# A token mixer on one core: softmax division moved behind the weighing of the values, and the work lists of three engines laid anew

## The chip, the core and the metric

The kernel runs on one core of one Trainium2 chip, in one launch. Its time is the device time in microseconds (us). The profile of one execution gives, for each engine, when every instruction ran and what it waited for. TensorE is called PE, VectorE DVE, ScalarE ACT, GpSimd POOL, and SyncE, which only starts transfers here, SP.

## The reference, cut to what matters

All data is float32. 16 images become 64 tokens each, 32 text tokens are set behind them (N = 96 tokens of D = 192 numbers, 16 samples), and two layers follow. The first has an attention with 12 heads of 8 numbers, within 4 segments of 24 tokens:

```python
qb, kb, vb = (blk(q), blk(k), blk(v))          # (B, H, SPLIT, seg, hd)
scores = jnp.einsum('bhsqd,bhskd->bhsqk', qb, kb) * scale
attn = jax.nn.softmax(scores, axis=-1)
ob = jnp.einsum('bhsqk,bhskd->bhsqd', attn, vb)
o = ob.transpose(0, 2, 3, 1, 4).reshape(B, N, C1)
return o @ W_proj + b_proj
```

Behind it come a residual sum, a layer norm and a mixture of 8 experts (192 to 768 to 192, two experts a token, a capacity for each expert). The second layer has a linear attention with L1 norms and a soft mixture of 8 experts with 4 slots each.

## The kernel before

**Staging.** The 1536 tokens are worked on in four rounds j = 0 to 3 of four samples (384 tokens, three blocks of 128). The stages follow one another on PE: patch embedding with the first attention (to about 123 us), the eight experts (to 246.5 us), the sums over experts and layer 1 (to the end). In the first and the last stage the rounds overlap: while round j's softmax runs on DVE and ACT, PE projects round j+1.

**Order.** There is no scheduler. Each engine has a list of calls, written out by hand (PE's begins at L917, ACT's at L1298, DVE's at L1866, POOL's at L450), and works it off strictly in that order. Calls wait for one another by semaphores; in PE's list the lines `free(name=count)` are such waits. A call that waits holds up everything behind it on its engine.

**The first attention, round j.** `turn_inputs` and `reduce_inputs` bring the normalised tokens in front of the projections `queries`, `keys`, `values`. `scores(j)` (L640) gives the logits of all 12 heads in three PSUM banks, one for each group g of four heads. DVE's `score_max(j, g)` subtracts the largest logit, ACT's `exp_scores(j, g)` takes the exponential, and DVE's `score_norm(j, g)` (L1541, L1543, L1545) adds up each row, takes the reciprocals of the sums and multiplies the weights by them. Then PE turns the weights (`turn_weights`, L647), ACT copies them to SBUF (`keep_weights`, L1208), and PE multiplies them with the values (`weigh_values(j, g)`, L658): 16 products of 24 columns for each g, all of one g into the same 32 rows of PSUM bank 3. ACT's `keep_outputs(j)` (L1213) copies the result, `project(j)` (L669) projects it, and DVE's `add_attention(j)` (L1568) adds it to the residual stream.

**Routing.** From there DVE works out each token's experts (`route_moments`, `route_logits`, `choose_first`, `choose`), PE counts the tokens of each expert (`count_choices`), DVE places them (`place`, L1625) and writes one-hot matrices (`mark_slots`, L1648), and PE's `dispatch` (L692) and `dispatch_tails` (L707) gather the experts' inputs. Only when all four rounds are dispatched does PE begin the experts (L718).

**Dummies.** `keep_busy` (L509) multiplies the identity with constants into a bank that is free. Four calls stand ahead of the experts, behind `dispatch(0)`, `turn_weights(3, 1)` and `count_choices(3)` (two); others stand in layer 1. The clock of PE can fall when it idles, and they fill waits.

**Transfers.** SP starts the weights of the first three experts in 12 pieces, each behind a number of subtractions of `score_max`; the later ones follow as buffers come free.

Of the kernel before, what the change touches and what calls it, by code (L numbers as in the profile page):

```python
# [5 lines left out]
ALU = mybir.AluOpType  # L6
# [3 lines left out]
AX_X = mybir.AxisListType.X  # L10
# [20 lines left out]
J, NB, QB = 4, 3, 32  # L31
# [58 lines left out]
def build(nc, xin, xhalo, txt, wtok, wtok2, lnw, lnb, tokbias, consts, wred, bred, wqkv0, bqkv0, wproj0, bproj0,  # L90
          wrouter, wi, wo, wq1, wkv1, wproj1, bproj1, slots, lscale, wdown, bdown, wup, bup, out):
    with ExitStack() as ctx:  # L92
# [68 lines left out]
        ssum = sb("ssum", [128, NGRP, 4 * GRP])  # L161
# [212 lines left out]
        def _(gp):  # L374
# [32 lines left out]
            for b in range(4):  # L407
                then(gp.memset(qmask[QB * b:QB * b + QB, b:b + 1], 1.0))
            for a in (0, 64):
# [79 lines left out]
        def _(pe):  # L489
# [154 lines left out]
            def turn_weights(j, g):  # L644
                pe.wait_ge(sem("a_prob"), NGRP * j + g + 1)
# [279 lines left out]
            square_sums(1)  # L925
# [7 lines left out]
            reduce_inputs(0)  # L933
            patches(2, 1)
# [7 lines left out]
            square_rows(3)  # L942
            free(tok_mid=4, tok_var=4)
            scores(0)
            turn_inputs(1)
            free(tok_mid=6, tok_var=6)
            patches(3, 0)
            free(a_sub=3)
            turn_projection()
            free(a_xnT=2)  # L950
            reduce_inputs(1)
# [3 lines left out]
            square_sums(3)  # L955
            turn_weights(0, 0)
            route_projection()
            queries(1)
            free(tok_mid=8, tok_var=8)
            values(1)  # L960
            free(a_kexp=8, a_qT=2)
            turn_inputs(2)
            free(a_vexp=9)
            turn_weights(0, 1)
# [6 lines left out]
            free(a_probT=2)  # L971
            weigh_values(0, 0)
            weigh_values(0, 1)
            weigh_values(0, 2)
# [8 lines left out]
            turn_weights(1, 0)  # L983
            turn_weights(1, 1)
            free(a_sub=6)
            scores(2)
            free(a_probT=5)
            weigh_values(1, 0)
            turn_inputs(3)
            free(a_vexp=27)  # L990
            count_choices(0)
            free(a_probT=4)
            turn_weights(1, 2)
            weigh_values(1, 1)
            weigh_values(1, 2)
            free(a_xnT=4)
            reduce_inputs(3)
            free(a_oT=2)
            project(1)
            free(a_h=2, r_part=2)  # L1000
            turn_weights(2, 0)
            free(r_counted=1)
            values(3)
            turn_weights(2, 1)
            queries(3)
            free(a_xl=4, a_xrT=4)
            keys(3)
            free(a_probT=8)
            weigh_values(2, 0)
            weigh_values(2, 1)  # L1010
            free(a_sub=9)
            scores(3)
            turn_weights(2, 2)
            free(a_vexp=36)
            count_choices(1)
            weigh_values(2, 2)
# [3 lines left out]
            free(r_counted=2)  # L1020
            free(xeT=2)
            keep_busy(0, 512)
# [19 lines left out]
            keep_busy(0, 384)  # L1042
            keep_busy(0, 256)
# [17 lines left out]
            combine(2, 0)  # L1061
            linear_keys_values(0, 0)
            linear_queries(0)
            linear_keys_values(0, 1)
            turn_linear(1)
# [6 lines left out]
            linear_keys_values(1, 1)  # L1072
            linear_outputs(0)
            linear_keys_values(1, 2)
            key_products(1)
            combine(3, 1)
            linear_queries(1)
            linear_project(0, 0)
            turn_linear(2)
            key_sums(1)  # L1080
# [7 lines left out]
            key_sums(2)  # L1088
            turn_linear(3)
            soft_logits(0)  # L1090
            linear_project(1, 0)
# [5 lines left out]
            linear_outputs(2)  # L1097
            turn_soft(1)
            linear_keys_values(3, 2)
            soft_logits(1)  # L1100
            linear_project(2, 0)
            linear_project(2, 1)
            linear_queries(3)
            soft_inputs(1)
            key_sums(3)
            key_products(3)
            keep_busy(0, 512, 2)
            linear_outputs(3)
            turn_soft(2)
            linear_project(3, 0)  # L1110
            soft_logits(2)
            linear_project(3, 1)
            soft_inputs(2)
            keep_busy(0, 256)
# [8 lines left out]
            soft_hidden(3, 4)  # L1123
            slot_outputs(2)
            token_outputs(0)
# [7 lines left out]
        def _(act):  # L1133
# [75 lines left out]

            def keep_outputs(j):  # L1210
                act.wait_ge(sem("a_oT_ps"), j + 1)
                need(act, "a_proj_ps", j - 2)
                nc.scalar.copy(oT[0:C1, j % 3].rearrange("c (x b t) -> c x b t", x=NB, b=4),  # L1213
# [934 lines left out]
```

## Time and profile before

| | |
|---|---|
| median of 3 runs | 353.9 us (352.41 to 355.89) |
| the profiled execution, its own time | 353.93 us |
| its span, first to last instruction | 352.1 us |
| PE busy | 329.2 us (93%) |
| DVE busy | 204.2 us (58%) |
| ACT busy | 100.9 us (29%) |
| POOL busy | 50.5 us (14%) |
| granted clock of PE, mean | 0.993 |

Busy time counts compute instructions only. A float32 product is two instructions in the trace. The groups of instructions name a line, an engine, the tiles, the shape, the count, the busy time, the mean of one in ns, and the idle time just before them with what ended it. A granted clock of 1.00 is 2.4 GHz, 0.50 is 1.2 GHz.

### The profile page before, as it was taken

The numbers are of one execution on the slowest core, as the hardware profiler recorded it, in microseconds if no ns is written. First come the engines' busy times: TensorE is split into PE (matmuls) and PEld (weight loads), VectorE is DVE, ScalarE is ACT, GpSimd is POOL, SyncE is SP. The second block draws the span as 40 slices with busy tenths as digits, with TensorE's granted clock in tenths as the row PEclk, the third lists the DMA queues.
The fourth block names the chain that finished last, engine by engine and source line by source line (L and its number), as shares of the span: only waits on it lengthen the run. The fifth ranks groups of instructions, "written<-read, shape, count | busy, mean of one in ns | idle before, by whom it ended". The sixth has DMA issues, their size and how long they took to land. (4 is left out here: it accounts for less than half of the span.)

```text
span 352.1 us, 7993 instructions
## 1 busy us (share of the span) xinstructions
PE 329.2 (93%) x3292; PEld 234.9 (67%) x3292; DVE 204.2 (58%) x639; ACT 100.9 (29%) x210; POOL 50.5 (14%) x119
## 2 busy tenths in 40 slices
PE   3899999998799899999999999999999999997975
PEld 3676567786574458678595867758867675775564
DVE  5936388999988952243325324332525476888545
ACT  1233557876433510101011010101021234322440
POOL 8604252332111020000000000000111020110100
PEclk9999999999999999999999999999999999999989
DMA  7993010522600029993487130000000000000005
GB/s 257 345 234 104 4 58 17 136 77 63 159 16 1 2 54 197 186 238 85 143 193 169 38 98 0 3 0 3 0 2 0 2 2 0 3 2 0 2 1 134
DMA packets 27804, 26.65 MB, mean 76 GB/s; under 512 B 4118, under 2 KB 22936, under 8 KB 27768
## 3 DMA queue, kind: packets, MB, share of 16 engines
q1 hardware_dynamic: 26871, 25.55, 29.0%
q10 hardware_dynamic: 896, 0.59, 0.7%
q8 instruction: 26, 0.43, 0.5%
q14 instruction: 11, 0.08, 0.1%
HBM read 24.86 MB, written 1.28 MB: 74 GB/s over the span
## 5 line engine op out<-in xcount | busy, mean ns | idle before, releaser
L736 PEld LDWEIGHTS banks<-sb_wo_sl,sb_attn_hidT_attn 128*128 128x128 f32 x384 | 62.2, 190 | 5.6 <-issue 4.9
L736 PE MATMUL banks<-sb_wo_sl,sb_attn_hidT_attn 128*128 128x192 f32 x384 | 64.5, 328 | 0.0
L1714 DVE COPY sb_w_tok_e_out<-banks 60x384 f32<-60x384 f32 x32 | 17.8, 555 | 49.8 <-PE banks L736 49.3
L1242 ACT ACTIVATE sb_attn_hidT_attn<-banks 128x480 f32<-128x480 f32 x24 | 13.6, 571 | 102.9 <-PE banks L723 102.9
L718 PE MATMUL banks<-sb_tok_xeT,sb_wi_sl 128*128 128x480 f32 x96 | 40.1, 567 | 1.1 <-ACT sb_tok_xeT L1227 1.1
L1704 DVE TENSOR_SCALAR sb_attn_hidT_attn<-banks 128x480 f32<-128x480 f32 x24 | 15.8, 658 | 27.9 <-PE banks L723 25.9
L718 PEld LDWEIGHTS banks<-sb_tok_xeT,sb_wi_sl 128*128 128x128 f32 x96 | 18.0, 190 | 18.9 <-issue 17.0
L503 PE MATMUL banks<-sb_tok_xeT 128*32 128x193 f32 (+1 forms) x512 | 24.8, 328 | 0.0
L723 PE MATMUL banks<-sb_tok_xeT,sb_wi_sl 64*128 64x480 f32 x96 | 21.5, 580 | 0.0
L503 PEld LDWEIGHTS banks<-sb_tok_xeT 128*32 128x32 f32 (+1 forms) x512 | 16.8, 109 | 6.5 <-issue 3.6
L474 POOL MEMSET sb_attn_hidT_attn<- 1x384 f32 x1 | 0.4, 413 | 119.6 <-PE banks L736 119.6
L779 PE MATMUL banks<-sb_w_kv,sb_xnT 96*128 96x384 f32 x48 | 17.3, 493 | 0.0
L756 PE MATMUL banks<-sb_w_tok_e_out,sb_onehot_combT 128*64 128x192 f32 x192 | 16.9, 329 | 0.1
L723 PEld LDWEIGHTS banks<-sb_tok_xeT,sb_wi_sl 64*128 64x128 f32 x96 | 8.6, 186 | 12.3 <-issue 12.3
L756 PEld LDWEIGHTS banks<-sb_w_tok_e_out,sb_onehot_combT 128*64 128x64 f32 x192 | 13.3, 137 | 3.2 <-issue 1.0
L658 PEld LDWEIGHTS banks<-sb_attn_hidT_attn 128*32 128x32 f32 x384 | 12.4, 113 | 2.9 <-ACT sb_attn_hidT_attn L1208 1.8
L1488 DVE BATCH_NORM_STATS2 sb_stat<-sb_h 128x6 f32<-128x192 f32 x48 | 14.0, 347 | 0.3
L658 PE MATMUL banks<-sb_attn_hidT_attn 128*32 128x24 f32 x384 | 13.2, 190 | 0.8 <-ACT sb_attn_hidT_attn L1208 0.8
L1141 ACT ACTIVATE sb_onehot_combT<-sb_tok_xeT 128x1024 f32<-128x1024 f32 x8 | 8.3, 1054 | 15.8 <-DMA sb_tok_xeT<-in_xhalo 15.8
L520 PE MATMUL banks<-sb_w_tok_e_out,sb_ln_b 128*128 128x192 f32 x30 | 7.3, 404 | 5.4 <-DMA sb_w_tok_e_out<-in_wtok 5.4
L242 PE MATMUL banks<-sb_cst,sb_attn_hidT_attn 128*128 128x128 f32 (+1 forms) x72 | 10.8, 280 | 1.7 <-DVE sb_logits L1571 1.2
L779 PEld LDWEIGHTS banks<-sb_w_kv,sb_xnT 96*128 96x128 f32 x48 | 8.5, 190 | 4.7 <-issue 0.4
(239 smaller groups left out, 540.1 us busy)
## 6 DMA issues: line engine op xcount, KB each, us to landing
sb_wo_sl<-in_wo SPq DMA_DIRECT2D x16, 288.0 KB, 4.1
sb_tok_xeT<-in_xin SPq DMA_DIRECT2D x8, 448.0 KB, 6.0
sb_onehot_combT<-route_rows SPq DMA_DIRECT2D x6, 512.0 KB, 8.8
sb_wi_sl<-in_wi SPq DMA_DIRECT2D x8, 288.0 KB, 3.4
sb_wi_sl<-in_wi SPq DMA_DIRECT2D x24, 96.0 KB, 3.4
sb_xn<-route_rows SPq DMA_DIRECT2D x4, 512.0 KB, 11.3
sb_w_tok_e_out<-in_wtok SPq DMA_DIRECT2D x2, 960.0 KB, 7.3
sb_attn_hidT_attn<-route_rows SPq DMA_DIRECT2D x2, 512.0 KB, 12.2
```

Source lines behind the costliest of these rows:

```text
L242: return nc.tensor.transpose(dst, src, ident[0:rows, 0:rows])
L503: nc.tensor.matmul(PS[QB * b:QB * b + QB, bank, at:at + D + 1], x_k[0:rows, (2 * j + b // 2) % NX, t, cols], w_eff[0:rows, t], start=(t == ...
L658: mm = nc.tensor.matmul(PS[g * 32:g * 32 + 32, 3, at:at + SEG], v_exp[:, j % 2, b, s, g * 32:g * 32 + 32], probT[:, g, b, s * 32:s * 32 + ...
L718: nc.tensor.matmul(PS[:, HID_BANKS[f], 0:SLOTS], wi_sl[:, q, f * 128:(f + 1) * 128], xeT[:, 0, e].rearrange("k g c -> k (g c)"), start=Tru ...
L723: nc.tensor.matmul(PS[:, HID_BANKS[2 * n + z], 0:SLOTS], wi_sl[rows, q, F + n * 128:F + (n + 1) * 128], xeT[rows, 1, e].rearrange("k g c - ...
L736: mm = nc.tensor.matmul(PS[:, 4 + j // 2, j % 2 * D:(j % 2 + 1) * D], hidT[:, e % 2, f, j * 128:(j + 1) * 128], wo_sl[:, q, f], start=(f = ...
L756: mm = nc.tensor.matmul(PS[rows, comb_bank(j, part), blk % 2 * D:(blk % 2 + 1) * D], combT[:, NB * j + blk, ep, rows], e_out[:, 2 * j + hf ...
L779: mm = nc.tensor.matmul(PS[:, 2 + blk, 0:2 * D], xnT[:, kh, blk * 128:(blk + 1) * 128], w_kv1[:, kh], start=(kh == 0), stop=(kh == 1))
L1242: nc.scalar.activation(hidT[:, e % 2, f].rearrange("f (g c) -> f g c", g=PAIRS)[:, :, 0:CAP], PS[:, HID_BANKS[f], 0:SLOTS].rearrange("f (g ...
L1488: ve.bn_stats(stat6[:, blk], h[:, j, blk]).then_inc(sem("stat6"), 1)
L1704: ve.tensor_scalar(hidT[:, e % 2, f].rearrange("f (g c) -> f g c", g=PAIRS)[:, :, 0:CAP], PS[:, HID_BANKS[f], 0:SLOTS].rearrange("f (g c) ...
L1714: ve.tensor_copy(e_out[64 * (e % 2):64 * (e % 2) + CAP, hf * 4 + z:hf * 4 + z + 3:2, e // 2], PS[64 * z:64 * z + CAP, 4 + hf, 0:2 * D].rea ...
```

## The change

1. **Division behind the weighing.** `score_norm` is gone. PE turns the bare exponentials (`turn_weights` waits for `a_exp`). `weigh_values(j)` first multiplies a new constant `head_ones` (128x32; ones where a row belongs to a head's keys) with the turned weights: three products of 384 columns, one for each g, which give each head's sum in PSUM bank 2, in the layout of the outputs. DVE's new `sum_scales(j)` takes the reciprocal of these 96x384 numbers, and `keep_outputs(j)`, now on DVE, multiplies the outputs by it while it copies them.
2. **Three head groups in one step.** `weigh_values(j)` waits once for all three groups, and its 48 products go over g innermost, so that three neighbours write different 32 rows.
3. **No dummies ahead of the experts.** The four `keep_busy` calls there are gone.
4. **Orders laid anew** on PE, ACT and DVE, in both layers. DVE gets one more wait, for `keys(1)`, ahead of `token_rows(6)`. POOL sets `head_ones` up (five fills).

```diff
-            def weigh_values(j, g):
-                if g == 0:
-                    pe.wait_ge(sem("a_vexp"), 9 * j + 9)
-                    pe.wait_ge(sem("a_vexp_late"), 2 * SEGS * (j + 1))
-                pe.wait_ge(sem("a_probT"), NGRP * j + g + 1)
+            def weigh_values(j):
+                pe.wait_ge(sem("a_vexp"), 9 * j + 9)
+                pe.wait_ge(sem("a_vexp_late"), 2 * SEGS * (j + 1))
+                pe.wait_ge(sem("a_probT"), NGRP * j + NGRP)
+                for g in range(NGRP):
+                    mm = nc.tensor.matmul(PS[g * 32:g * 32 + 32, 2, 0:TOK], head_ones[:],
+                                          probT[:, g].rearrange("k b (s t) -> k b s t", s=SEGS)[:, :, :, 0:SEG],
+                                          start=True, stop=True)
+                mm.then_inc(sem("a_total_ps"), 1)
                 for b in range(4):
                     for s in range(SEGS):
                         at = b * N + s * SEG
-                        mm = nc.tensor.matmul(PS[g * 32:g * 32 + 32, 3, at:at + SEG], v_exp[:, j % 2, b, s, g * 32:g * 32 + 32],
-                                              probT[:, g, b, s * 32:s * 32 + SEG], start=True, stop=True)
-                if g == NGRP - 1:
-                    mm.then_inc(sem("a_oT_ps"), 1)
+                        for g in range(NGRP):
+                            rows = slice(g * 32, g * 32 + 32)
+                            mm = nc.tensor.matmul(PS[rows, 3, at:at + SEG], v_exp[:, j % 2, b, s, rows],
+                                                  probT[:, g, b, s * 32:s * 32 + SEG], start=True, stop=True)
+                mm.then_inc(sem("a_oT_ps"), 1)
...
-            def score_norm(j, g):
-                n = NGRP * j + g
-                ve.wait_ge(sem("a_exp"), n + 1)
-                ve.tensor_reduce(ssum[:, g], prob_view(j, g), AX_X, ALU.add).then_inc(sem("a_sum"), 1)
-                ve.wait_ge(sem("a_sum"), 2 * n + 1)
-                ve.reciprocal(ssum[:, g], ssum[:, g]).then_inc(sem("a_sum"), 1)
-                ve.wait_ge(sem("a_sum"), 2 * n + 2)
-                ve.tensor_tensor(prob_view(j, g), prob_view(j, g), ssum[:, g].unsqueeze(2).to_broadcast(every_key), ALU.mult
-                                 ).then_inc(sem("a_prob"), 1)
+            def sum_scales(j):
+
+                ve.wait_ge(sem("a_total_ps"), j + 1)
+                ve.reciprocal(o_scale[:], PS[0:C1, 2, 0:TOK]).then_inc(sem("a_sum"), 1)
+
+            def keep_outputs(j):
+                ve.wait_ge(sem("a_sum"), j + 1)
+                need(ve, "a_proj_ps", j - 2)
+                ve.wait_ge(sem("a_oT_ps"), j + 1)
+                ve.tensor_tensor(oT[0:C1, j % 3].rearrange("c (x b t) -> c x b t", x=NB, b=4),
+                                 PS[0:C1, 3, 0:TOK].rearrange("c (b x t) -> c x b t", b=4, x=NB),
+                                 o_scale[:].rearrange("c (b x t) -> c x b t", b=4, x=NB), ALU.mult).then_inc(sem("a_oT"), 1)
```

PE's list around the last two rounds, and DVE's around `project(3)`:

```diff
-            free(r_counted=2)
-            free(xeT=2)
-            keep_busy(0, 512)
             free(a_h=3, r_part=3)
             turn_weights(3, 0)
             turn_weights(3, 1)
-            keep_busy(0, 256)
-            free(a_probT=11)
-            weigh_values(3, 0)
+            free(r_counted=2)
+            free(xeT=2)
             free(a_probT=10)
             turn_weights(3, 2)
-            weigh_values(3, 1)
-            weigh_values(3, 2)
             count_choices(2)
+            weigh_values(3)
             free(a_oT=4)
             project(3)
...
             count_choices(3)
-            keep_busy(0, 384)
-            keep_busy(0, 256)
             dispatch(2)
...
             mark_slots(1)
+            sum_scales(3)
             place(2)
-            route_norm(2)
+            keep_outputs(3)
             add_attention(3)
```

In layer 1, PE's list moves `linear_keys_values(1, 2)` and `combine(3, 1)` ahead of `key_products(1)`, and `turn_soft(2)` and `soft_logits(2)` ahead of `linear_project(3, 0)`; DVE's moves `soft_norm(2)` ahead of `norm_products(3)`, `slot_weights(2)` ahead of `add_linear(3, 0)`, and each `token_shift` up to its `soft_max`.

## Rows read from the trace of the kernel before

**Rows 1.** The page's first line: the span of the profiled execution.

```profile
span 352.1 us, 7993 instructions
```

**Rows 2.** Windows by stage: busy us of PE, PEld, DVE, ACT, POOL; PEclk; DMA.

```profile
44.00:122.76 78.76, 72.92 (x1300) 50.47 (x1289) 71.21 (x255) 44.64 (x111) 19.43 (x52) 1.00 0.22 59
122.76:246.50 123.74, 123.74 (x576) 88.56 (x576) 43.63 (x83) 13.60 (x24) 1.90 (x2) 1.00 0.47 100
246.50:349.20 102.70, 95.60 (x823) 70.07 (x822) 64.81 (x226) 27.94 (x55) 10.61 (x13) 0.98 0.04 10
```

**Rows 3.** Timeline of PE: start us, length us, instruction, count, [idle before it].

```profile
42.02 1.05 PE L565 MATMUL banks<-sb_onehot_combT,sb_cst 128*32 128x256 f32 x16
44.94 1.32 PE L640 MATMUL banks<-sb_attn_hidT_attn,sb_qT 32*32 32x96 f32 x96
...
92.03 1.29 PE L669 MATMUL banks<-sb_w_px,sb_oT 105*128 105x208 f32 x6 [0.66 <-ACT sb_oT L1213]
...
97.15 1.10 PE L509 MATMUL banks<-sb_cst 128*128 128x512 f32 x2 [1.21 <-ACT sb_tok_xeT L1227]
...
98.96 0.60 PE L509 MATMUL banks<-sb_cst 128*128 128x256 f32 x2
...
104.56 1.30 PE L669 MATMUL banks<-sb_w_px,sb_oT 105*128 105x208 f32 x6
...
111.90 1.32 PE L509 MATMUL banks<-sb_cst 128*128 128x384 f32 x4
...
122.76 5.10 PE L718 MATMUL banks<-sb_tok_xeT,sb_wi_sl 128*128 128x480 f32 x12 [1.11 <-ACT sb_tok_xeT L1227]
```

**Rows 4.** Groups by line, 30 to 124 us: busy us, mean ns, idle before.

```profile
L658 PE MATMUL banks<-sb_attn_hidT_attn 128*32 128x24 f32 x384 | 13.2, 190 | 0.8 <-ACT sb_attn_hidT_attn L1208 0.8
L1545 DVE TENSOR_TENSOR sb_attn_hidT_attn<-sb_attn_hidT_attn,sb_ssum 128x384 f32<-128x384 f32 x12 | 6.7, 561 | 0.4
L1541 DVE TENSOR_REDUCE sb_ssum<-sb_attn_hidT_attn 128x16 f32<-128x384 f32 x12 | 6.5, 546 | 0.4 <-ACT sb_attn_hidT_attn L1202 0.3
L1213 ACT COPY sb_oT<-banks 96x384 f32<-96x384 f32 x4 | 1.9, 476 | 2.8 <-PE banks L658 2.8
```

**Rows 5.** Groups by line, whole span: RECIPROCAL on DVE by size.

```profile
L1543 DVE RECIPROCAL sb_ssum<-sb_ssum 128x16 f32<-128x16 f32 x12 | 3.0, 253 | 0.4
L1836 DVE RECIPROCAL sb_c_st<-sb_c_st 128x3 f32<-128x3 f32 x4 | 0.7, 179 | 0.1
L1822 DVE RECIPROCAL sb_d_st<-sb_d_st 128x1 f32<-128x1 f32 x4 | 0.6, 158 | 2.7 <-ACT sb_attn_hidT_attn L1280 2.7
L1634 DVE RECIPROCAL sb_r_sums<-sb_r_sums 128x12 f32<-128x12 f32 x1 | 0.2, 229 | 0.0
```

**Rows 6.** Timeline of DVE: one score_norm; the work of round 2.

```profile
57.50 0.55 DVE L1541 TENSOR_REDUCE sb_ssum<-sb_attn_hidT_attn 128x16 f32<-128x384 f32 x1
...
58.85 0.74 DVE L1480 SCALAR_TENSOR_TENSOR sb_h<-sb_tok_mid,sb_tok_stat,sb_bias_row 128x192 f32<-128x192 f32 x2
...
94.06 0.75 DVE L1568 TENSOR_TENSOR sb_h<-sb_h,banks 128x576 f32<-128x576 f32 x1
...
101.63 1.79 DVE L1648 TENSOR_TENSOR sb_onehot_combT<-sb_cst,sb_slot_of 128x480 f32<-128x480 f32 x3
```

**Rows 7.** Timelines of POOL and PE in the setup.

```profile
11.59 0.20 POOL L416 COPY sb_tok_xeT<-sb_cst 128x8 f32<-128x8 f32 x1
...
15.69 0.35 PE L535 MATMUL banks<-sb_tok_xeT,sb_cst 128*32 128x192 f32 x1 [1.10 <-DVE sb_tok_xeT L1446]
```

**Rows 8.** Windows and PE timeline: the granted clock behind a wait.

```profile
338.00:340.00 2.00, 2.00 (x11) 2.00 (x11) 0.46 (x1) 0.00 (x0) 0.00 (x0) 0.50 0.00 0
...
337.42 2.87 PE L874 MATMUL banks<-sb_attn_hidT_attn 128*96 128x128 f32 x12 [2.21 <-DVE sb_attn_hidT_attn L1829]
```

**Rows 9.** Timelines of PE and of DVE in layer 1.

```profile
277.47 1.27 PE L803 MATMUL banks<-sb_attn_hidT_attn 32*96 32x96 f32 x48 [0.57 <-ACT sb_attn_hidT_attn L1257]
...
325.33 0.87 DVE L1488 BATCH_NORM_STATS2 sb_stat<-sb_h 128x6 f32<-128x192 f32 x3
```

More of the change, by code:

```diff
@@ L408, in _ @@
                 then(gp.memset(qmask[QB * b:QB * b + QB, b:b + 1], 1.0))
+            then(gp.memset(head_ones[:], 0.0))
+            for r in range(GRP):
+                then(gp.memset(head_ones[32 * r:32 * r + 32, HDIM0 * r:HDIM0 * r + HDIM0], 1.0))
             for a in (0, 64):
@@ L1088, in _ @@
             key_sums(2)
+            linear_project(1, 0)
+            soft_logits(0)
             turn_linear(3)
-            soft_logits(0)
-            linear_project(1, 0)
             linear_project(1, 1)
@@ L1208, in keep_weights @@
                 nc.scalar.copy(probT[:, g].rearrange("k b t -> k (b t)"), PS[:, 2 + g % 2, 0:512]).then_inc(sem("a_probT"), 1)
[L1210 to L1213, printed above, removed]
-                               PS[0:C1, 3, 0:TOK].rearrange("c (b x t) -> c x b t", b=4, x=NB)).then_inc(sem("a_oT"), 1)
             def exp_routes(j):
@@ L1881, in _ @@
             token_rows(5)
+            score_max(0, 0)
             token_write(4)
-            score_max(0, 0)
             score_max(0, 1)
-            score_max(0, 2)
             token_write(5)
             first_moments(2)
-            score_norm(0, 0)
-            score_norm(0, 1)
+            score_max(0, 2)
             first_norm(2)
+            ve.wait_ge(sem("a_k_ps"), 2)
             token_rows(6)
@@ L1893, in _ @@
             keep_projection()
-            score_norm(0, 2)
             token_write(6)
@@ L1899, in _ @@
             score_max(1, 1)
+            sum_scales(0)
+            keep_outputs(0)
+            first_norm(3)
             score_max(1, 2)
-            score_norm(1, 0)
-            first_norm(3)
-            score_norm(1, 1)
             add_attention(0)
@@ L1908, in _ @@
             choose(0)
-            score_norm(1, 2)
             score_max(2, 0)
             score_max(2, 1)
-            route_norm(0)
-            score_max(2, 2)
-            place(0)
-            score_norm(2, 0)
-            add_attention(1)
-            score_norm(2, 1)
-            route_moments(1)
-            mark_slots(0)
-            route_logits(1)
-            score_norm(2, 2)
-            choose_first(1)
-            scale_routes(0)
-            choose(1)
+            place(0)
+            sum_scales(1)
+            keep_outputs(1)
+            score_max(2, 2)
+            add_attention(1)
+            route_moments(1)
+            route_logits(1)
+            route_norm(0)
+            choose_first(1)
+            choose(1)
+            scale_routes(0)
+            mark_slots(0)
             score_max(3, 0)
+            place(1)
             score_max(3, 1)
-            place(1)
-            score_max(3, 2)
-            score_norm(3, 0)
-            add_attention(2)
-            score_norm(3, 1)
-            route_moments(2)
-            scale_routes(1)
+            sum_scales(2)
+            keep_outputs(2)
+            scale_routes(1)
+            add_attention(2)
+            route_moments(2)
+            score_max(3, 2)
             route_logits(2)
-            score_norm(3, 2)
             choose_first(2)
+            choose(2)
             route_norm(1)
-            choose(2)
             mark_slots(1)
+            sum_scales(3)
             place(2)
-            route_norm(2)
+            keep_outputs(3)
             add_attention(3)
@@ L1947, in _ @@
             choose(3)
+            route_norm(2)
             route_norm(3)
+            place(3)
             scale_routes(3)
-            place(3)
             mark_slots(2)
```

202 lines of the change are left out of this document (97 added, 105 removed).

## The prediction

> **What bounds the kernel now.** I read the page's first lines, then windows by stage, then the timelines of PE and DVE through the first attention, then the groups by line. The span is 352.1 us [rows 1], and what lies around it in the profiled execution is 1.8 us (353.93 by its own time), so that execution stands on the median of 353.9. From 122.76 to 246.5 us PE is busy without a gap: the experts, untouched by the change, waiting for no weights. What the change can move lies on either side: the 78.8 us from 44 to 122.76 and the 102.7 us behind the experts [rows 2]. In the first of these two engines are nearly full: PE 72.9 us, DVE 71.2 us. PE idles 5.8 us there, in single waits of about 1 us, each for a result that ACT or DVE had just made [rows 3]. So neither engine alone is the bound. A round goes scores, softmax, turning, weighing, `project`, routing, and its hand-overs between PE and DVE set the pace as soon as one becomes longer. That is how the change must be read: how much work leaves, and how long the new hand-over is.
>
> **Work that leaves PE.** The 384 instructions of the weighing take 13.2 us [rows 4], 34 ns apart, all of one group into the same 32 rows. With g innermost three neighbours write different rows. The nearest row is `scores`: 96 instructions to different tiles in 1.3 us, 13.7 ns apart [rows 3]. By that a round's weighing takes 1.3 us instead of 3.3; the other end is 3.3, if nothing overlaps. I take 1.4. The three products for the sums: `square_rows` (L565), 16 instructions of 256 columns over four sets of rows, two deep, takes 1.05 us [rows 3]. One set's pair of instructions of 256 columns is about 0.49 us, of 384 columns then 0.7. Three side by side are 0.7 us, one behind the other 2.1; I take 0.7. For four rounds: 13.2 goes, 4 x 2.1 = 8.4 comes. The dummies lasted 1.10, 0.60 and 1.32 us with overlaps [rows 3], 2.8 us of PE's list. PE's work falls by 13.2 - 8.4 + 2.8 = 7.6 us.
>
> **Work that leaves DVE.** A `score_norm` takes 1.35 us from its start to the next call's [rows 6]; twelve are 16.2 us. What comes is four times a multiplication of 96x384, which is 0.55 us by its equal L1545 [rows 4], or 0.5 from start to start, and four times a reciprocal of 96x384 numbers. No such instruction is in the trace, and this is the price the forecast hangs on. Its small relatives take 158 ns for 1 number a row, 179 for 3, 229 for 12 and 253 for 16 [rows 5]: 95 ns for 15 more numbers, 6.3 ns each. A plain pass over 384 numbers takes 0.55 us [rows 4], that is 1 ns each on top of the 0.15 of the smallest. At 6.3 ns, 384 numbers are 2.5 us. The low end is 0.55, were the reciprocal of a long row a plain pass; the high end is 3.4, were each number eight plain steps (8 x 1.05 ns, and 0.15). I take 2.5, the value that the rows extrapolate to. DVE's work then falls by 16.2 - 4 x 3.0 = 4.2 us, a quarter of what leaves; the division is of 384 numbers a row where it was of 48.
>
> The rows so far show 6.3 ns per number. The Trainium skill ("VectorE: DVE Perf Modes", the walkthrough of the 8-slice pipeline) says the reciprocal is an iterative division whose step is repeated eight times. That speaks against the change: if the eight repetitions were eight plain steps, it is rival D; if they partly overlap, it fits the measured 6.3 ns.
>
> **ACT and POOL.** ACT loses four copies (1.9 us [rows 4]); ACT was waiting much of the stage (44.6 of 78.8 us busy [rows 2]), so this counts nothing. POOL's five more fills, about 1 us if each is like the 0.20 of L416, stand ahead of L416, which ends at 11.8 us and is first needed by the patches behind the PE instruction of 15.69 us [rows 7]: covered by 3.9 us. Without that cover they would cost their 1 us.
>
> **The new hand-over.** Before, the way from the last value product to `project` was one ACT copy: 0.66 us of waiting at `project(2)`, none at `project(3)`, where `count_choices` filled it [rows 3]. Now it is 2.5 + 0.5 us on DVE, of which the 1.4 us of value products cover a part, and it starts only when DVE comes to it. Behind `sum_scales` on DVE stand `keep_outputs`, `add_attention` and the whole routing of the round; behind `project` on PE stand the turning of the next round and `dispatch`. I walked the lists of after call by call, each call as long as in the trace, start to start, with the three new prices:
> - round 0: the earlier part is a little late (`keys(1)` 1.1 us, because `score_max(0, 0)` now stands ahead of `token_write(4)` and waits for `scores(0)`), the weighing wins that back and ends at 65.5; `project(0)` waits 0.9 us.
> - round 1: value products end at 76.9, a shade earlier than before; DVE comes to the sums 0.65 us late; `project(1)` starts at 79.15 after 2.3 us of idle PE.
> - round 2: value products end at 91.7. The sums are ready at 90.25, but DVE is at `score_max(3, 1)` until 91.3 (it had waited 1 us for `count_choices(1)`). Reciprocal to 93.8, outputs to 94.3: `project(2)` starts at 94.4, where it was 92.03 [rows 3], with 2.7 us of idle PE.
> - round 3: DVE's work from `add_attention(2)` to the end of `mark_slots(1)` took 9.3 us [rows 6]; less two `score_norm`, plus one `score_max` (1.07), it is 7.7, so it ends at 103.5 with the sums ready since 102.6. Reciprocal to 106.05, `place(2)` 0.63, outputs 0.5: `project(3)` starts at 107.25 instead of 104.56 [rows 3], with 3.2 us of idle PE.
> - from `project(3)` to the experts it was 18.2 us [rows 3]. The removed dummies (1.32 us) do not shorten this: DVE's routing, to the last `mark_slots`, sets it. I get 18.05, and the experts start at 125.3, 2.5 us later.
>
> The books agree roughly: PE's idle time goes from 5.8 to 15.1 us (+9.3), its work falls by 7.6, which makes +1.7. I take the middle, +2.2 us, for the first attention.
>
> **Layer 1.** PE works 95.6 of 102.7 us here [rows 2], so a reordering can win only waits. `key_products(1)` waited 0.57 us for ACT [rows 9], and two calls now stand ahead of it. `soft_logits(2)` comes a projection earlier, so `slot_weights(2)` does too, and the chain that sets the end starts at the moments of round 3 (325.33 [rows 9]), perhaps 0.2 us earlier. I take -0.8 us, between 0 and -2, with a loss of 1 possible, since every moved call has others behind it.
>
> **The sum.** 353.9 + 2.2 - 0.8 = 355.3 us, by the profiled execution and by the median alike.
>
> **The rivals.**
> - A, as above: 355.3, by itself 352.5 to 357.8. Chance 0.43.
> - B, the other side: the reciprocal of long rows is a plain pass, or is covered. For it speaks only that no row has more than 16 numbers; against it the even slope of four sizes. At 0.55 us each hand-over shortens by 1.95, `project(1)` comes 2.6 us earlier than in A, `project(2)` 4.7, `project(3)` 6.8, and the experts start at 118.5: 349.0 us. Between the two prices the time moves 3.4 us for each us of reciprocal, so below about 2.0 us the change is a gain, and below 1.0 one of over 1%. Chance 0.22, part of it for a walk that overrates the waits.
> - C, the clock: in the trace PE waited 2.21 us before the products at 337.42, and from 338 to 340 us the granted clock was 0.50, 1.2 GHz [rows 8]. The 12 instructions there took 2.87 us, and half of that, 1.4, is what the halved clock costs them. A's waits of 2.3, 2.7 and 3.2 us are as long, and the dummies are gone. With what stands behind those 12, a fall costs about 1.7 us where PE sets the pace; two that count are +3.4: 358.7 us. Against it: the whole stage from 44 to 122.76, with waits of up to 1.21 us, kept its 1.00 [rows 2, 3], and nothing says that two fall where PE sets the pace. Chance 0.20.
> - D, a dearer reciprocal, eight plain steps a number, 3.4 us: 0.9 x 3.4 = +3.1, 358.4 us. Against it stands the slope of rows 5, 6.3 ns where this needs 8.4. Chance 0.08.
> - E, the change doesn't do what it says: products of neighbouring groups do not overlap. Then a round's weighing is 3.3 and the sums 2.1 us; PE has 4 x 3.3 = 13 us more, of which the waits take about half: 362. `scores` and the patches, which overlap in the same way, speak against it. Chance 0.03. The rest, 0.04, is a loss or gain in layer 1 of another size.
>
> The granted clock of 0.50 at 338 us [rows 8] is the lower of two levels. The Trainium skill ("TensorE: Matmul & The Clock Gate", Part 1) says that the array falls to half speed when it has been idle and comes back when it has been busy, and here the trace agrees.
>
> **The numbers.** The forecast is A's, 355.3 us. B at the low end and C at the high end together with D make the range 349 to 360; it leaves out E and what is beyond B. Within 1% (3.5 us) is about what a measurement of this kernel can tell from no change. Faster by over 1% is B: 0.21. Slower by over 1% is C, most of D and E, and A's upper edge: 0.33. Within 1%: 0.46.
>
> **What would show it.** In the profile of after: the reciprocal of 96x384, at 2.4 to 2.6 us (0.6 is B, 3.4 is D). The value products 96 in 1.3 to 1.6 us a round (3.3 is E). Waits of PE at L669 of 2 us and more for DVE in rounds 1 to 3; if they are under 1 us the walk is wrong. The first expert product at 125, not 118 or 128. A granted clock under 1 between 80 and 115 us is C. Behind the experts, the stretch to the end at 102 us. I am wrong above all if DVE reaches the sums sooner than in my walk.

## The result, and the profile after

The changed kernel is slower. Its median is 364.29 us over four executions (363.69 to 367.66), against 354.84 (352.41 to 355.89) for the kernel before on the same chip: 1.030 times as long, 95% interval 1.025 to 1.035. The forecast was 355.3, with a range up to 360.

The profiled execution took 364.78 us, 10.9 more than the 353.93 of before, and its span is 363.0 us. First the page of after: its first line, the busy times, and the granted clock in 40 slices of 9 us. In before the clock's row holds nines only, but for one 8 near the end; here the slice from 64 to 73 us and the five from 82 to 127 are an 8 or a 7.

```profile
span 363.0 us, 7999 instructions
...
PE 331.4 (91%) x3308; PEld 232.4 (64%) x3308; DVE 200.9 (55%) x611; ACT 99.0 (27%) x206; POOL 50.1 (14%) x124
...
PEclk9999999898788899999999999999999999999989
```

The windows of after by stage (columns as in [rows 2]):

```profile
44.00:133.91 89.91, 74.47 (x1316) 47.29 (x1308) 68.36 (x231) 43.02 (x107) 18.53 (x52) 0.89 0.18 52
133.91:257.65 123.74, 123.74 (x576) 88.56 (x576) 43.55 (x82) 13.69 (x24) 1.90 (x2) 1.00 0.50 100
257.65:360.10 102.45, 95.41 (x823) 70.54 (x822) 64.88 (x226) 27.62 (x55) 10.81 (x13) 0.98 0.04 10
```

Beside [rows 2] this places the loss. The first attention takes 89.91 us where it took 78.76, +11.15. The experts take the same 123.74. The last stage takes 102.45 where it took 102.70. The sum, 10.9, is the whole difference.

Inside the first attention, PE's idle time is 89.91 - 74.47 = 15.4 us, and the forecast had 15.1. Its busy time is what went another way: the forecast had 72.9 - 7.6 = 65.3 us, and it is 74.5. The clock is the reason. Its mean over the stage is 0.89: (1 - 0.89) x 89.91 / 0.5 = 20 us of the stage ran at 1.2 GHz. By estimate, that is up to 10 us more for the same work.

The groups of after, 30 to 134 us, show that the prices of the single operations were those forecast, and the waits of PE, 60 to 134 us (total us, times, longest), where it stood:

```profile
L1528 DVE RECIPROCAL sb_o_scale<-banks 96x384 f32<-96x384 f32 x4 | 10.2, 2551 | 0.9 <-PE banks L659 0.9
L668 PE MATMUL banks<-sb_attn_hidT_attn 128*32 128x24 f32 x384 | 5.3, 195 | 0.0
L659 PE MATMUL banks<-sb_attn_hidT_attn,sb_head_ones 128*32 128x384 f32 x24 | 4.0, 583 | 0.0
L1534 DVE TENSOR_TENSOR sb_oT<-banks,sb_o_scale 96x384 f32<-96x384 f32 x4 | 2.2, 554 | 0.1
```

```profile
PE banks L678 <- DVE sb_oT L1534: 9.0, 4, 2.8
PE banks L701 <- DVE sb_onehot_combT L1638: 1.6, 1, 1.6
PE banks L243 <- ACT sb_attn_hidT_attn L1205: 1.5, 2, 1.2
PE banks L727 <- ACT sb_tok_xeT L1218: 1.3, 1, 1.3
```

L678 is `project`. The reciprocal is 2.55 us, and the value products, 13.2 us before [rows 4], are 5.3. The four waits at `project` are 9.0 us together; the walk had 0.9 + 2.3 + 2.7 + 3.2 = 9.1. The timeline of PE in after shows them one by one, with what came behind:

```profile
67.81 1.70 PE L678 MATMUL banks<-sb_w_px,sb_oT 105*128 105x208 f32 x6 [1.52 <-DVE sb_oT L1534]
...
81.19 1.43 PE L678 MATMUL banks<-sb_w_px,sb_oT 105*128 105x208 f32 x6 [2.49 <-DVE sb_oT L1534]
...
98.52 1.69 PE L678 MATMUL banks<-sb_w_px,sb_oT 105*128 105x208 f32 x6 [2.16 <-DVE sb_oT L1534]
100.13 3.94 PE L701 MATMUL banks<-sb_onehot_combT,sb_xn 64*128 64x480 f32 x12
...
112.33 1.84 PE L678 MATMUL banks<-sb_w_px,sb_oT 105*128 105x208 f32 x6 [2.80 <-DVE sb_oT L1534]
114.10 3.78 PE L701 MATMUL banks<-sb_onehot_combT,sb_xn 64*128 64x480 f32 x12
...
129.92 2.69 PE L701 MATMUL banks<-sb_onehot_combT,sb_xn 64*128 64x480 f32 x12
133.91 5.10 PE L727 MATMUL banks<-sb_tok_xeT,sb_wi_sl 128*128 128x480 f32 x12 [1.30 <-ACT sb_tok_xeT L1218]
```

The same twelve products of `dispatch` (L701) take 2.69 us at 129.92 and 3.94 and 3.78 behind the waits of rounds 2 and 3. Windows of 4 us of after (granted clock third from the end of each line):

```profile
68.00:72.00 4.00, 4.00 (x40) 2.66 (x39) 3.86 (x16) 1.20 (x3) 0.00 (x0) 0.57 0.33 95
80.00:84.00 4.00, 2.81 (x9) 2.09 (x10) 3.34 (x9) 0.52 (x1) 0.00 (x0) 0.78 0.23 63
84.00:88.00 4.00, 3.90 (x17) 2.28 (x16) 3.79 (x26) 2.67 (x6) 1.11 (x2) 0.80 0.31 95
92.00:96.00 4.00, 4.00 (x92) 3.05 (x95) 2.62 (x7) 1.49 (x3) 0.61 (x3) 0.57 0.28 78
100.00:104.00 4.00, 4.00 (x13) 1.57 (x13) 3.59 (x16) 0.00 (x0) 1.11 (x2) 0.66 0.39 104
112.00:116.00 4.00, 3.67 (x12) 2.28 (x14) 1.94 (x8) 0.00 (x0) 0.00 (x0) 0.62 0.00 0
124.00:128.00 4.00, 4.00 (x20) 1.80 (x20) 3.91 (x8) 0.55 (x2) 0.00 (x0) 0.68 0.02 4
```

Six falls to 1.2 GHz, of about 3.4 us each: one behind each wait at `project`, one at 92 to 96 us behind two waits of only 0.60 and 0.89 us, one at 123 to 127 us behind the 1.58 us wait of `dispatch`. Without the clock the forecast's walk gives 125.3 for the first expert product. It is at 133.91, so the clock would be 8.6 of the 11.15 us, and the new hand-over 2.5. That is a reading; the experiments test it.

### The profile page after: what moved, and what is told of

The parts are those of the page before. It is cut to its first block, busy times and chain, and to the rows that moved or that the text cites. A ratio compares the mean times of both kernels' runs of the same rounds, so it can differ in the third digit from the quotient of the medians.

```text
span 363.0 us, 7999 instructions
## 1 busy us (share of the span) xinstructions
PE 331.4 (91%) x3308; PEld 232.4 (64%) x3308; DVE 200.9 (55%) x611; ACT 99.0 (27%) x206; POOL 50.1 (14%) x124
## 4 chain that ended last, share of the span: by engine, by line
PE 77%; DVE 10%; issue 5%; ACT 4%; DMA 2%; SPq 0%; POOLq 0%; POOL 0%; DVEq 0%; ACTq 0%
PE banks L745 18%; PE banks L727 11%; PE banks L507 6%; PE banks L732 6%; PE banks L788 4%; PE banks L765 4%; PE banks L701 3%; PE banks L243 3%; DVE sb_o_scale L1528 3%; PE banks L798 2%; PE banks L614 2%; PE banks L678 2%; DMA sb_w_tok_e_out<-in_wtok 2%; PE banks L716 1%; DVE sb_tok_xeT L1433 1%
## 5 line engine op out<-in xcount | busy, mean ns | idle before, releaser
L701 PE MATMUL banks<-sb_onehot_combT,sb_xn 64*128 64x480 f32 x48 | 14.8, 762 | 1.6 <-DVE sb_onehot_combT L1638 1.6
L678 PE MATMUL banks<-sb_w_px,sb_oT 105*128 105x208 f32 x24 | 6.7, 425 | 9.0 <-DVE sb_oT L1534 9.0
L243 PEld LDWEIGHTS banks<-sb_cst,sb_attn_hidT_attn 128*128 128x128 f32 (+1 forms) x72 | 8.3, 140 | 7.1 <-issue 6.1
L243 PE MATMUL banks<-sb_cst,sb_attn_hidT_attn 128*128 128x128 f32 (+1 forms) x72 | 10.9, 283 | 1.7 <-ACT sb_attn_hidT_attn L1205 1.5
```

The source lines that it names most:

```text
L243: return nc.tensor.transpose(dst, src, ident[0:rows, 0:rows])
L678: mm = nc.tensor.matmul(PS[:, 2 + blk // 2, blk % 2 * 256:blk % 2 * 256 + PX], oT[:, j % 3, blk * 128:(blk + 1) * 128], w_px[:], start=Tru ...
L701: mm = nc.tensor.matmul(PS[:, banks[hf], 0:E * CAP], xn2[rows, j, blk, 0:128], onehot[rows, j % 2, blk], start=(blk == 0), stop=(blk == NB ...
```

## The experiments

Each ratio is to the kernel before, run on the same chip: median 355.06 us in 25 executions (for the dummies in all the waits, the removed dummies put back, the dummies taken away, no reciprocal), 354.34 in 17 (for the division on ACT with and without dummies, the three groups alone, layer 1) and 354.00 in 7 (for the dummies in one wait, the dummies at the end too, the three groups taken out).

### The hand-over or the clock

**Dummies in the waits.** After, with 41 small products (the identity with 128 columns of constants, into a free bank) at the places where PE's list waits, so many at each that they end about when the wait does: 6, 9, 8 and 11 ahead of the four `project`, 3 behind `scores(3)` ahead of `count_choices(1)`, 4 behind `turn_weights(3, 1)`. The two `keep_busy` of before stand ahead of `dispatch(2)` again, and two `free` lines guard the bank that the dummies write. All else is as in after, the division too.

```diff
+            def hold_clock(times, bank=1):
+                for _ in range(times):
+                    nc.tensor.matmul(PS[:, bank, 0:128], ident, cst[:, 0:128], start=True, stop=True)
...
             weigh_values(3)
+            hold_clock(11)
             free(a_oT=4)
             project(3)
```

> The changed kernel with 41 dummy products of 128 columns (0.2 us each) set into PE's waits: 6, 9, 8 and 11 ahead of the four waits for the divided outputs, 3 ahead of the wait for the values of round 3, 4 ahead of the third turning of round 3, and the two old ones ahead of dispatch(2). The hand-over stays as it is. Theory 'clock' (the waits of the longer hand-over are as walked, and the rest of the loss is PE at half clock behind them): the granted clock stays at 1.00 up to the experts, they start at 125 to 127 us instead of 133.9, and the time is 355 to 357.5 us. Rival 'hand-over' (the waits alone make the loss, the clock only slows work that would have waited): the clock stays up and the time stays at 362 to 365. Rival 'dummies in the way': PE is late by them, 358 to 362.

Measured: 356.29 us, 1.003 times before (1.001 to 1.005). The dummies give back 8.0 us of after's 364.3. In its timeline of PE `project` of rounds 1 to 3 stands where the walk of the prediction had put it (79.15, 94.4, 107.25), and its window up to the experts keeps a clock of 1.00:

```profile
67.32 1.29 PE L683 MATMUL banks<-sb_w_px,sb_oT 105*128 105x208 f32 x6 [0.19 <-DVE sb_oT L1549]
...
79.42 1.29 PE L683 MATMUL banks<-sb_w_px,sb_oT 105*128 105x208 f32 x6 [0.63 <-DVE sb_oT L1549]
...
94.92 1.29 PE L683 MATMUL banks<-sb_w_px,sb_oT 105*128 105x208 f32 x6 [1.26 <-DVE sb_oT L1549]
...
107.63 1.29 PE L683 MATMUL banks<-sb_w_px,sb_oT 105*128 105x208 f32 x6 [0.19 <-DVE sb_oT L1549]
...
126.07 5.10 PE L732 MATMUL banks<-sb_tok_xeT,sb_wi_sl 128*128 128x480 f32 x12 [1.26 <-ACT sb_tok_xeT L1233]
```

```profile
44.00:126.07 82.07, 75.89 (x1383) 52.75 (x1375) 67.88 (x228) 42.61 (x106) 18.85 (x52) 1.00 0.19 57
```

So most of the loss is the clock's: the same hand-overs, with PE kept at work during them, cost 3.3 us before the experts (126.07 against 122.76), and with the clock left to fall they cost 11.15. The difference, 7.8 us, is what the run gives for the falls, where the walk gave 8.6.

The 1.003 flatters the kernel a little. Its ten executions are five at a mean clock of 0.998 to 1.000 and about 355.5 us, and five at 0.994 to 0.995 and about 356.9. Executions of before with these clocks have medians of 352.8 and 354.2, so at equal clock the kernel is 2.7 us slower than before.

**Dummies in one wait only.** The same with nothing but the 11 dummies ahead of `project(3)`.

> The changed kernel with dummies at one wait alone: 11 products of 128 columns ahead of the wait for the outputs of round 3. Theory 'clock', one fall at a time: only the fall at 112.8 to 116.3 us goes, which has PE setting the pace (project(3), dispatch(1)) with half of 3.4 us to lose: 1.5 to 1.8 us off, 361.5 to 363.5 us. If the falls are linked (a shorter stage, another fall elsewhere), it is 364 as before.

Measured: 361.70 us, 1.022 (1.016 to 1.029), 2.6 less than after. The fall at 112 to 116 us is gone, as the theory had it, but two others are missing too: this profile has three falls in the stage (at 80 to 84, 97 to 101 and 121 to 125 us) where after's has six. None comes at 68 to 72 us behind the same wait of 1.53 us, which lies ahead of all the dummies, so they can't be the reason there. The experts begin at 130.92. The fall at the dummies' own wait is gone; what one fall is worth, this run doesn't show, since the falls also vary from execution to execution (mean clock 0.967 to 0.981), and the intervals of the two kernels overlap.

**Only the removed dummies put back.** After, with `keep_busy` again behind `free(xeT=2)` (512 and 256 columns) and ahead of `dispatch(2)` (384 and 256).

> The changed kernel with the four removed dummies put back, the first two behind the wait for the experts' inputs of round 0, the other two ahead of dispatch(2). They stand at none of the four waits for the divided outputs. Theory 'clock': they can only prevent the fall at 122 to 126 us (1.7 us at most); 362 to 364.5 us, five falls of the clock left. Rival 'the removed dummies are the loss': 355 to 358 us.

Measured: 362.09 us, 1.021 (1.016 to 1.027). The fall ahead of the experts is gone (1.00 from 120 us on), but the others have grown: one at 81 us, one stretch at 1.2 GHz from 91 to 101, one from 112 to 119. Two of its windows of 4 us:

```profile
92.00:96.00 4.00, 3.62 (x105) 2.55 (x104) 3.33 (x6) 0.52 (x1) 0.00 (x0) 0.50 0.41 111
96.00:100.00 4.00, 2.48 (x8) 1.98 (x8) 1.45 (x4) 0.00 (x0) 0.00 (x0) 0.50 0.74 222
```

Together that is again 20 us at half clock, and the experts begin at 133.58, 0.3 us earlier than in after. So the old dummies, which stand at the wrong places for the new waits, give nothing before the experts in this profile; the 2.2 us in the medians are within the intervals of the two kernels.

**Only the dummies taken away.** Before, without its four `keep_busy` ahead of the experts.

> The kernel before with only its four dummies ahead of the experts taken out. Its waits there are 0.2 to 1.2 us. If the dummies held the clock: one or two falls between 95 and 120 us, 355 to 357 us. If they did nothing: PE's list is 2.8 us shorter, but DVE's routing sets the end of the stage: 352.5 to 354.5 us, without a fall. I take the second.

Measured: ten executions in two groups, six of 352.94 to 354.87 us with a mean clock of 0.990 to 0.994, and four of 360.38 to 361.88 with 0.965 to 0.971. The six stand at 0.998 of before (0.994 to 1.002). Its profile is of the first group, with the experts at 122.64 us. None of before's 49 executions is above 358.7. In six of ten executions the four dummies are worth nothing, as the prediction had it. The other four are 6 us longer at a lower clock; no trace of one was kept, and that the missing dummies make them so is not shown.

### The price of the division

**No reciprocal.** After, with a plain copy in its place, so that the outputs are scaled by the sums and not divided by them.

```diff
-                ve.reciprocal(o_scale[:], PS[0:C1, 2, 0:TOK]).then_inc(sem("a_sum"), 1)
+                ve.tensor_copy(o_scale[:], PS[0:C1, 2, 0:TOK]).then_inc(sem("a_sum"), 1)
```

> The changed kernel with a plain copy of the sums in place of the reciprocal, so that the outputs are multiplied by the sums and not divided: this part of the computation is changed. The copy should take 0.5 us where the reciprocal takes 2.55. Theory 'clock': each wait for the outputs falls under 1 us, the clock stays up nearly everywhere, and the experts start at 118.5 to 120: 348.5 to 351 us. Rival 'hand-over without clock': the walk of the prediction gives 3.4 us for each us of reciprocal, 7 us off: 357 us.

Measured: 352.06 us, 0.993 (0.990 to 0.996). The waits at `project` are 0, 1.18, 1.25 and 1.37 us, one fall is left in the stage (mean clock 0.75 and 0.82 in the windows from 108 to 116 us, behind the 1.58 us wait of `dispatch`), and the experts begin at 121.01. 2 us off each reciprocal gave 12.2 us. The walk without the clock had rated this at 6.8 us (experts at 118.5 instead of 125.3); the rest goes with the falls, one where after has six. Rival B's world would have been a gain of 0.7%, not of 1.4%.

**The division on ACT.** After, with 1/x as the exponential of minus the logarithm, on ACT, which has half its time free.

```diff
+            def sum_scales(j):
+                act.wait_ge(sem("a_total_ps"), j + 1)
+                nc.scalar.activation(o_scale[:], PS[0:C1, 2, 0:TOK], ACT.Ln).then_inc(sem("a_sum"), 1)
+                act.wait_ge(sem("a_sum"), 2 * j + 1)
+                nc.scalar.activation(o_scale[:], o_scale[:], ACT.Exp, scale=-1.0).then_inc(sem("a_sum"), 1)
```

> The changed kernel with the reciprocal of the sums taken off DVE: ACT makes it in two passes of 96x384, the logarithm and the exponential of its negative, which stand in ACT's list behind the copies that free it (rounds 0 to 3: behind the router part, the turned inputs and the last two turned weights). By ACT's rows of 96x384 (0.48 us) that is 1.0 us instead of 2.55, and DVE's list is 10.2 us shorter. Theory 'clock': the waits for the outputs fall under 1.3 us as with the copy, the experts start at 119 to 121.5 us, 349 to 352.5 us, faster than the kernel before by about 1%. Rival 'ACT is late': ACT stands at another call when the sums are ready, the waits stay near 2 us and the clock falls, 355 to 360 us. If the logarithm and the exponential needed their tables loaded anew (1.3 us each as at the end of the kernel), it would be over 360.

Measured: 351.85 us, 0.992 (0.988 to 0.995). The timeline of ACT in round 0 shows the pair; from start to end it takes 1.04 us where the reciprocal took 2.55:

```profile
65.45 0.49 ACT L1209 ACTIVATE sb_o_scale<-banks 96x384 f32<-96x384 f32 x1
65.97 0.52 ACT L1211 ACTIVATE sb_o_scale<-sb_o_scale 96x384 f32<-96x384 f32 x1
```

The waits at `project` are 0.72 to 0.92 us, the fall at 108 to 116 us is left (0.80 and 0.77), and the experts begin at 120.67.

**The division on ACT and dummies.** The same with nine small dummies (one ahead of each of the four `project`, 2 behind `scores(3)`, 3 behind `turn_weights(3, 1)`), and the two `keep_busy` ahead of `dispatch(2)`.

> The same with one dummy product ahead of each wait for the outputs, two ahead of the values' wait, three ahead of the third turning of round 3 and the two old ones ahead of dispatch(2). If the clock still falls once or twice without them (as it did once with the plain copy, 110 to 114 us), this takes 1 to 3 us off and narrows the spread between executions: 348 to 351 us. If no fall is left, the same time as without.

Measured: 348.21 us (347.76 to 348.66), 0.982 (0.978 to 0.986): faster than both kernels, and the best here. Its timeline of PE at the experts:

```profile
118.49 5.10 PE L732 MATMUL banks<-sb_tok_xeT,sb_wi_sl 128*128 128x480 f32 x12 [1.26 <-ACT sb_tok_xeT L1239]
```

No fall is left in the stage. The mean clock of its four executions is 0.999, where the kernel without the dummies has 0.984 to 0.995. The experts begin 2.2 us earlier, and the medians differ by 3.6 us.

**Dummies at the end too.** The same with seven instead of three dummies of 512 columns ahead of the last long wait of layer 1.

> The kernel with the reciprocal on ACT and dummies at the waits, and seven dummies of 512 columns instead of three ahead of soft_inputs(3), where PE waits 2.20 us in every kernel of this study and the clock then falls in some executions and not in others. The four more take 1.9 us. Where the clock would have fallen: 1 to 1.5 us less; where not: the same. Expected 347 to 348.3 us against 348.2, with less spread.

Measured: 349.12 us, 0.986 (0.980 to 0.992). No gain over the one above, whose clock was already whole in every execution. The seven dummies last longer than the wait that they fill: the products behind them have no wait and start 1.1 us later than in the kernel above (333.84 us, where they stand at 332.72 behind a wait of 2.20). So filling a wait that brings no fall gains nothing, and dummies that outlast it cost their excess.

### The three groups in one step

**Alone, in before.** Before, with one weighing a round, its 48 products with g innermost; the division stays in `score_norm`, and all dummies stay.

> The kernel before with only part 2: one weighing step a round, groups side by side, the weights still divided ahead of it, everything else and all dummies as they were. The weighing should take 1.2 us instead of 3.3 a round, 8 us of PE's list. If PE's list set the pace: 345 to 348 us. If the hand-overs between PE and DVE set it: 352 to 355.5 us, PE's saved time turning into waits (and, where they are long enough, a fall of the clock). I take the second.

Measured: 357.89 us, 1.009 (1.005 to 1.012). I had expected 352 to 355.5, a gain or nothing. The products are as short as in after, but the first weighing now waits for all three groups of weights, and `scores(3)` waits for ACT's copies of the keys (L1176), a time that the weighing of two groups (2.10 us) had filled in before. Timeline of PE, and windows:

```profile
64.88 1.21 PE L659 MATMUL banks<-sb_attn_hidT_attn 128*32 128x24 f32 x96 [2.09 <-ACT sb_attn_hidT_attn L1200]
...
88.45 1.31 PE L640 MATMUL banks<-sb_attn_hidT_attn,sb_qT 32*32 32x96 f32 x96 [2.38 <-ACT sb_attn_hidT_attn L1176]
```

```profile
64.00:68.00 4.00, 3.12 (x101) 2.55 (x102) 3.78 (x11) 3.44 (x8) 1.15 (x3) 0.82 0.87 245
...
92.00:96.00 4.00, 3.32 (x102) 3.16 (x102) 2.52 (x8) 1.31 (x3) 0.00 (x0) 0.50 0.86 249
```

The 8 us that leave PE's list become waits, the longest of 2.1 and 2.4 us, the clock falls behind these two, and the experts begin at 127.31, 4.6 us later than in before. The stage's mean clock is 0.92, so by the estimate used above up to 6.7 us of it are half-clocked work: with the clock held, this part might have been no loss. No run shows that.

**Taken out of after.** After, with g outermost in the value products again, one group behind the other.

> The changed kernel with part 2 undone in its main point: still one weighing step, but all products of one group behind the other, as before. By the prediction's rival E this costs PE 2 us a round. Theory 'clock': the reciprocal runs meanwhile and sets the hand-over, PE is busy 3.2 us where it was busy 1.2 and idle 2.2, so each wait falls to 0.3 to 1 us and the clock stays up: 356 to 359 us, faster than the changed kernel although PE works 8 us more. If PE's work counted: 366 to 372 us.

Measured: 360.51 us, 1.018 (1.012 to 1.024). PE has 7 us more to do (2.99 us a round instead of 1.2), and the kernel is 3.8 us faster than after. The waits at `project` are 0, 1.17, 0.81 and 1.52 us, four windows of 4 us have a clock under 1 instead of ten, and the experts begin at 128.90. The long products were filling the hand-over. I had expected 356 to 359; two falls are left. The one at 118 to 122 us stands behind a wait of 1.58 us. The other begins at 91 us, with nothing longer ahead of it than 0.60 and 0.90 us, as in after. Timeline of PE, and the window behind it:

```profile
87.14 1.32 PE L644 MATMUL banks<-sb_attn_hidT_attn,sb_qT 32*32 32x96 f32 x96 [0.60 <-ACT sb_qT L1174]
89.35 0.42 PE L686 MATMUL banks<-sb_choice,sb_count_masks 128*128 128x48 f32 x2 [0.90 <-ACT sb_attn_hidT_attn L1194]
```

```profile
92.00:96.00 4.00, 3.44 (x86) 3.34 (x84) 3.16 (x3) 0.52 (x1) 0.00 (x0) 0.73 0.55 164
```

### Layer 1

**Its new orders alone, in before.**

> The kernel before with only the lists of layer 1 (behind the sums over experts) taken from the changed kernel. The profile of after has 102.45 us from the first of these sums to the last value, before 102.70: 354.5 to 355.5 us beside 355, no difference that can be measured. The prediction had -0.8.

Measured: 352.48 us (352.00 to 353.88), 0.995 (0.993 to 0.997): 1.9 us faster, where I had expected no difference that shows. The clocks of the executions split this. At a mean clock of 0.994 to 0.995 three executions of this kernel are at 353.8 to 353.9, and the 25 such of before have a median of 354.2: the order itself is worth about 0.4 us. The other seven are at 0.998 to 1.000 and 352.0 to 352.8. So the larger part is a fall that mostly fails to come. It is the one at the last wait ahead of `soft_inputs(3)`; the timelines of PE, of this kernel and of after, show the same wait and two lengths of what follows ([rows 8] has 2.87 for before):

```profile
337.28 1.55 PE L874 MATMUL banks<-sb_attn_hidT_attn 128*96 128x128 f32 x12 [2.20 <-DVE sb_attn_hidT_attn L1829]
```

```profile
348.15 2.63 PE L883 MATMUL banks<-sb_attn_hidT_attn 128*96 128x128 f32 x12 [2.20 <-DVE sb_attn_hidT_attn L1819]
```

Twelve of the thirteen profiles have this wait of 2.20 or 2.21 us. In four of them the twelve instructions behind it take 1.55 or 1.56 us, in eight 1.90 to 2.87. The wait does not bring the fall for certain.

## Why the prediction was wrong

**The prices were right.** Reciprocal 2.5 us, measured 2.55: the slope of four small sizes carried to a row 24 times as long as the largest of them. Value products 1.4, measured 1.2. Sums 0.7, measured 0.64 to 0.67 where the clock was whole. A multiplication 0.5 to 0.55, measured 0.55. Rivals D and E were not what happened, nor was B.

**The walk was right, with some luck in its sums.** With the clock held, `project` of rounds 1 to 3 is 0.3, 0.5 and 0.4 us later than walked and the experts 0.8 us. The kernel is at 356.3 where 355.3 was forecast; at equal clock it is 2.7 us slower than before, where the sum had 2.2 - 0.8 = 1.4. Idle time of PE in the stage is 15.4 us in after, 15.1 forecast, and the waits at `project` add up to 9.0, 9.1 walked, but the single ones were off both ways: 1.52, 2.49, 2.16 and 2.80 against 0.9, 2.3, 2.7 and 3.2. The one that was walked too short, at `project(0)`, has the first fall behind it.

**The step that failed is the clock, rival C.** The forecast left the clock out of its sum. Rival C had the right mechanism, most of the place (a clock under 1 between 80 and 115 us; it was 68 to 127) and 0.20 of the chance, and it priced two falls of 1.7 us, +3.4. There were six, and with the clock held the experts begin 7.8 us earlier (8.6 by the walk). Three things were wrong in it:
- The number. Rows 8 had one wait of 2.21 us with a fall behind it. The walk gave three waits of that length and one of 0.9, and each should have been counted, with its neighbours: after the first fall the slower PE hands its results on later.
- The argument against. That the stage of before, "with waits of up to 1.21 us, kept its 1.00", was true and said nothing on waits of 2.5 us. It was also a statement on a PE that is busy 72.9 of 78.8 us; in the forecast's own books it was to be busy 65.3 of 81. Here the first fall came behind a wait of 1.52 us, in the two kernels with the lighter division the one fall left came behind 1.58, and the fall at 92 us had only 0.60 and 0.89 ahead of it. The argument would not have held for waits of the old length either.
- "Nothing says that two fall where PE sets the pace." In this stage most of PE's work is on the path: up to 10 us of slower work cost 7.8.

The Trainium skill ("TensorE: Matmul & The Clock Gate", "A second HAM failure mode: psum-queue depth-cycling") tells of a kernel whose frequent short idle times make the clock go back and forth, with the loss paid between bursts. The windows of after agree on the going back and forth, with six falls in 90 us. They differ on where the loss lies: PE's idle time is as forecast, and it is the products that take longer (`dispatch` 3.94 us and 2.69).

**The removed dummies** were costed at nothing, because DVE's routing hides their 1.32 us. As time they are hidden: without them before's six faster executions are at 0.998, and put back into after they move the experts by 0.3 us. As cover for the clock their worth is open: in after one fall goes and others grow, and why four executions in ten of before are 6 us longer without them is not shown.

**Shorter work as a gain.** The sum booked 8 us off PE's weighing against longer waits, and got +2.2. The two runs on it say that this part on its own loses (0.9%, 3 us, in before), and that taking it out of after gains 3.8 us. PE's list was not the bound where it was cut; the cut became idle time, and falls of the clock stood behind it.

**Layer 1.** Forecast -0.8, between 0 and -2. The stage is 0.25 us shorter in the profiles; measured alone it is -1.9, of which 0.4 is the order at equal clock. The forecast had only waits in mind, and of those -0.8 was twice too much.

**Its other sums.** B's own walk gives 355.3 - 6.8 = 348.5 us, not 349.0, and C and D together give 361.8 by their own prices, above the 360 of the range. Neither changes the outcome, which lies above both.

**The part that pays.** With the reciprocal off DVE and nine small dummies, the same change is at 348.2 us. What the change removed from DVE and PE was real; it was given back by an instruction of 2.55 us in a hand-over that PE's list does not fill, and by the falls behind it.

**Still open.** Which wait brings a fall in a given execution. In the first attention of these profiles a fall began in or behind each of the nine waits of 2.0 us and more that PE met at full clock, behind six of the nine of 1.5 to 1.6 us, and behind the pair of 0.60 and 0.90 us at `scores(3)` and `count_choices(1)` in three kernels of six. So I can count waits that may bring one, and not forecast which will. Open too is what the new orders of the first attention are worth by themselves: no run has them alone. And no trace shows where the clock fell in the four long executions of before without its dummies; their mean clock alone is known.

## What to carry to other kernels

Where a walk gives PE new waits of 1.5 us and more in a stage that was dense, price a fall of the clock for each of them, and make that the forecast, not a rival; shorter waits are no proof against one. Fill such waits with small dummy products that don't outlast the wait, or shorten the hand-over by moving its longest instruction to the engine with time to spare. Work taken from an engine is a gain only where that engine sets the pace; measure the part alone before it goes into a larger change.

## What the runs showed of the hardware that I had not expected

- Each of the six falls in after's first attention lasts about 3.4 us; in two other kernels one stretch at 1.2 GHz lasts from 91 to 101 us, three times as long. A half-clocked stretch of 3.4 us lowers the mean clock of this span by 0.0048, so the mean clock counts such stretches. Before's 49 executions stand in steps: 3 at 1.000 with a median of 352.8 us, 25 at 0.994 to 0.995 with 354.2, 20 at 0.989 to 0.990 with 355.7, one at 0.981 with 358.7. So the spread of this kernel's times goes with the number of its falls, about 1.4 us each. After's four executions are at 0.976, 0.972, 0.966 and 0.953, with 363.7, 363.8, 364.8 and 367.7 us.
- 1/x as logarithm and exponential on ACT takes 0.49 + 0.52 us for 96x384 numbers, where DVE's reciprocal takes 2.55, and in the timeline the second starts 0.03 us behind the first, so no table is loaded between them. The Trainium skill ("ScalarE: Activation LUTs", "Table sets: the hidden batching unit") lists one set of tables that holds both functions; the trace agrees.
- Products of 24 columns into three different groups of 32 rows start 12.5 ns apart (96 in 1.2 us), where the same products into one group are 31 to 34 ns apart (96 in 2.99 us, [rows 4]).
